# Two layers of cross attention on one core: transposes of the probabilities moved ahead of the filling matmuls, their copies between the two heads of a pair

## What is computed

```python
q = x @ Wq + bq; k = ctx @ Wk + bk; v = ctx @ Wv + bv          # layer 0
attn = softmax(q k^T * 16 ** -0.5 + mask)                       # 32 heads
y = layernorm(attn v @ Wo + bo + x) * gamma + beta
a = layernorm(ctx)                                              # layer 1
out = y + tanh(gate) * (softmax((y Wq) (a Wk)^T * 32 ** -0.5) (a Wv)) Wo
```

## Time and profile before

| | |
|---|---|
| median of 3 runs | 1230.87 us (1230.49 to 1233.23) |
| profiled execution: time / span | 1232.87 us / 1231.1 us |
| PE busy | 1151.5 us (94% of the span) |
| PEld busy | 942.6 us (77%) |
| DVE busy | 806.0 us (65%) |
| ACT busy | 749.8 us (61%) |
| POOL busy | 251.5 us (20%) |
| mean granted TensorE clock | 0.990 |
| DMA | 153.77 MB, mean 125 GB/s |

### The profile page before, as it was taken

One profiled execution on the slowest core, in us unless ns is written; L12 is line 12 of the kernel. 1 busy time (PEld: TensorE's weight loads), 2 busy tenths in 40 slices (PEclk: granted clock), 3 DMA queues, 4 the chain that ended last, 5 costly groups with the idle time before them and its releaser, 6 DMA issues.

```text
span 1231.1 us, 32229 instructions
## 1 busy us (share of the span) xinstructions
PE 1151.5 (94%) x10003; PEld 942.6 (77%) x10003; DVE 806.0 (65%) x2386; ACT 749.8 (61%) x2163; POOL 251.5 (20%) x264
## 2 busy tenths in 40 slices
PE   4989999999999999999999999999999999999997
PEld 4678778786877778787777878778787877878786
DVE  4365666767576776757677675766767586676735
ACT  3374656747475674747567474765747476574744
POOL 1041212111131211113121121312122131211210
PEclk9699999999999999999999999999999999999999
DMA  7665536547363654726365472735647273564500
GB/s 237 163 181 112 155 74 151 133 97 189 72 161 85 139 143 88 196 67 167 86 132 151 88 194 59 174 89 121 156 93 184 63 171 84 125 166 92 142 8 8
DMA packets 77821, 153.77 MB, mean 125 GB/s; under 512 B 10384, under 2 KB 47056, under 8 KB 77152
## 3 DMA queue, kind: packets, MB, share of 16 engines
q1 hardware_dynamic: 77792, 153.40, 51.3%
HBM read 113.72 MB, written 39.65 MB: 125 GB/s over the span
## 4 chain that ended last, share of the span: by engine, by line
PE 72%; issue 13%; ACT 6%; DVE 4%; DMA 1%; POOL 1%; DVEq 1%; ACTq 1%; SPq 0%; POOLq 0%
PE PJ L363 16%; PE TP L414 13%; PE OA L434 5%; PE SCO L400 5%; PE SCO L680 5%; PE SCO L458 4%; PE PJ L466 4%; ACT PR L1050 4%; PE PJ L376 4%; PE SCO L404 4%; PE OA L439 3%; PE SCO L363 2%; DVE SCO L824 2%; ACT PT L1061 1%; PE SCO L665 1%
## 5 line engine op out<-in xcount | busy, mean ns | idle before, releaser
L1050 ACT ACTIVATE PR<-SCO,MN 100x361 f32<-100x361 f32 x768 | 426.5, 567 | 144.8 <-DVE MN L824 143.2
L824 DVE CUSTOM_DVE_ANT_0 SCO<-SCO,MK 100x361 f32<-100x361 f32 x768 | 399.7, 551 | 126.0 <-PE SCO L400 99.7
L414 PEld LDWEIGHTS TP<-ident,PR 100*128 100x128 f32 x2304 | 222.5, 141 | 79.4 <-ACT PT L1061 28.5
L414 PE MATMUL TP<-ident,PR 100*128 100x100 f32 x2304 | 270.0, 253 | 6.7 <-ACT PT L1061 4.4
L1061 ACT ACTIVATE PT<-TP 121x600 f32<-121x600 f32 x256 | 172.2, 672 | 57.1 <-PE TP L414 55.1
L400 PE MATMUL SCO<-K0S,Q0S 128*100 128x362 f32 x512 | 165.8, 374 | 37.4 <-ACT PR L1050 36.1
L1050 ACT ACTIVATION_READ_ACCUMULATOR PR<-SCO,MN 100x1 f32 x768 | 159.7, 208 | 0.0
L834 DVE COPY PT<-TP 121x600 f32<-121x600 f32 x128 | 100.2, 783 | 65.6 <-PE TP L414 62.0
L400 PEld LDWEIGHTS SCO<-K0S,Q0S 128*100 128x100 f32 x512 | 74.8, 167 | 62.3 <-ACT PR L1050 60.0
L824 DVE DVE_READ_ACCUMULATOR2_ANT MN<- 100x1 f32 x768 | 108.5, 141 | 0.0
L1215 POOL TENSOR_TENSOR K1F<-K1F,KB 128x364 f32<-128x364 f32 x64 | 50.8, 794 | 259.8 <-DVE K1F L816 259.8
(11 more groups left out here) (140 smaller groups left out, 1814.8 us busy)
## 6 DMA issues: line engine op xcount, KB each, us to landing
K1S<-k_scr SPq DMA_DIRECT2D x128, 364.0 KB, 6.1
k_scr<-K1HL SPq DMA_DIRECT2D x64, 364.0 KB, 3.2
Q0S<-q_scr SPq DMA_DIRECT2D x128, 100.0 KB, 4.0
K0S<-k_scr SPq DMA_DIRECT2D x64, 182.0 KB, 5.0
AT<-ctx_cols SPq DMA_DIRECT2D x16, 722.0 KB, 9.4
V<-ctx_rows SPq DMA_DIRECT2D x16, 484.0 KB
q_scr<-QHL SPq DMA_DIRECT2D x16, 400.0 KB, 2.5
k_scr<-K1HL SPq DMA_DIRECT2D x32, 182.0 KB, 3.0
```

Of the source, the lines that this page charges most:

```text
L414: last = pe.transpose(TP[:, k % 2, c * T:(c + 1) * T], PR[0:T, k % NPR, c * SP:c * SP + P], ident[0:T, 0:T])
L824: dve.tensor_tensor_reduce(out=bank, in0=bank, in1=mask[0:T, :], scale=scale, scalar=3.4e38, op0=ALU.add, op1=ALU.min, accum_out=MN[0:T, k ...
L1050: act.activation(PR[0:T, k % NPR, 0:S], SCO[0:T, k % 3, 0:S], ACT.Exp, bias=MN[0:T, k:k + 1], scale=-1.0, accum_out=SM[0:T, k:k + 1]).then ...
```

## The change

1. PE, layer 0: the transposes of pair p-2 are issued directly behind the two scores of step p, ahead of its filling.
2. PE, layer 1: the second score of a step directly follows the first, then come the transposes, then the K1 matmuls.
3. DVE: its copies stand between the two shifts of a step, and one step earlier in the program (pair p-2 in step p), so that the copy of pair 21 is in step 23 of its own batch. The scalings K1F of steps 0, 3, 17 and 20 stand behind both shifts.
4. ACT: the copy of pair p-3 in layer 0 stands between the two exponentials of step p. The cast of chunk 3 of the keys moves from step 4 to step 5.
5. The bias of the layer-0 values is added by ACT in `values0_copied`, where it is one value per partition (BV0C, loaded by a DMA of its own at the start, counted by l_sm). The write to V0P is then a plain copy (`values0_out`) on ACT, ahead of its two Q1S copies; DVE no longer has it, and waits for the transposed values (v0_tr) ahead of K1F of chunk 0 instead.

```diff
         ROWS = sb("ROWS", [P, P + 3 * D + 1])
-        BV0, BO0, G0, B0 = (ROWS[:, 0:P], ROWS[:, P:P + D], ROWS[:, P + D:P + 2 * D], ROWS[:, P + 2 * D:P + 3 * D])
+        BO0, G0, B0 = ROWS[:, P:P + D], ROWS[:, P + D:P + 2 * D], ROWS[:, P + 2 * D:P + 3 * D]
...
+        BV0C = sb("BV0C", [P, 1])
...
             sp.dma_start(COLS[:, :], columns).then_inc(l_sm, 16)
+            sp.dma_start(BV0C[:, :], rows[0:P].rearrange("(p o) -> p o", o=1)).then_inc(l_sm, 16)
...
                         score(b, k)
+                    if p >= 2:
+                        transpose_probs(b, p - 2)
+                    elif not first:
+                        transpose_probs(b - 1, NPAIR - 2 + p)
                     if p in PV1_TAIL and not first:
...
                         out1(b - 1, range(*OUT1_STEPS[p]))
-                    if p >= 2:
-                        transpose_probs(b, p - 2)
-                    elif not first:
-                        transpose_probs(b - 1, NPAIR - 2 + p)
...
                     score(b, 2 * p)
+                    if p > 16:
+                        pe.wait_ge(prob, NH * b + 2 * p - 1)
+                    if p == 16:
+                        pe.wait_ge(rep_dve, 2 * b + 1)
+                    elif p == 17:
+                        pe.wait_ge(rep_dve, 2 * b + 2)
+                    score(b, 2 * p + 1)
+                    if p >= 18:
+                        transpose_probs(b, p - 2)
                     if more and p in K1_EARLY:
...
                     elif not more:
                         repeated_keys(3)
-                    if p > 16:
-                        pe.wait_ge(prob, NH * b + 2 * p - 1)
...
-                    score(b, 2 * p + 1)
...
-                    if p >= 18:
-                        transpose_probs(b, p - 2)
...
-            def values0(q, bank=PJ[:, 1, :]):
-                dve.wait_ge(v0_tr, q + 1)
-                dve.tensor_tensor(V0P[0:SP, :, :, HD0:2 * HD0],
...
                 if m == 0:
+                    dve.wait_ge(v0_tr, b + 1)
                     dve.wait_ge(rs_ev, b + 1)
...
                 for p in range(L0P):
-                    if p % 4 == 0 and (p > 0 or not first):
-                        if p > 0:
-                            probs_out(b, p - 3)
-                        else:
-                            probs_out(b - 1, NPAIR - 3)
-                    elif p == 2 and not first:
-                        probs_out(b - 1, NPAIR - 1)
                     if first and p in (4, 6, 8, 10):
                         keys1_scaled(b, p // 2 - 2)
-                    elif not first and p == 0:
+                    shift(b, 2 * p)
+                    if p == 1 and not first:
+                        probs_out(b - 1, NPAIR - 1)
+                    elif p % 4 == 3:
+                        probs_out(b, p - 2)
+                    shift(b, 2 * p + 1)
+                    if not first and p == 0:
                         keys1_scaled(b, 2)
                     elif not first and p == 3:
                         keys1_scaled(b, 3)
-                    for k in (2 * p, 2 * p + 1):
-                        shift(b, k)
...
-                probs_out(b, 13)
...
-                if more:
-                    values0(b + 1)
                 dve.wait_ge(mk1_b, b + 1)
                 for p in range(L0P, NPAIR):
-                    if p in (20, 22):
-                        probs_out(b, p - 3)
                     shift(b, 2 * p)
+                    if p in (19, 21, 23):
+                        probs_out(b, p - 2)
+                    shift(b, 2 * p + 1)
                     if more and p == 17:
                         keys1_scaled(b + 1, 0)
                     elif more and p == 20:
                         keys1_scaled(b + 1, 1)
-                    shift(b, 2 * p + 1)
...
-                act.activation(V0T[:, :], bank[:, 0:SC * SP], ACT.Copy).then_inc(v0_t, 1)
+                act.activation(V0T[:, :], bank[:, 0:SC * SP], ACT.Identity, bias=BV0C[:, 0:1]).then_inc(v0_t, 1)
+
+            def values0_out(q, bank=PJ[:, 1, :]):
+                act.wait_ge(v0_tr, q + 1)
+                act.activation(V0P[0:SP, :, :, HD0:2 * HD0],
+                               bank[0:SP, 0:SC * P].rearrange("p (s h d) -> p s h d", s=SC, h=KVH), ACT.Copy)\
+                    .then_inc(v0_ev, 1)
...
                     if p > 0:
                         exps(b, 2 * p - 2)
+                        if p >= 3 and (p - 3) % 4 != 1:
+                            probs_out(b, p - 3)
+                        elif p == 1 and not first:
+                            probs_out(b - 1, NPAIR - 2)
                         exps(b, 2 * p - 1)
...
-                    if p >= 3 and (p - 3) % 4 != 1:
-                        probs_out(b, p - 3)
-                    elif p == 1 and not first:
-                        probs_out(b - 1, NPAIR - 2)
...
-                    elif not first and p == 4:
+                    elif not first and p == 5:
                         keys1_high(b, 3, first)
...
                     .then_inc(q1_h, 1)
+                if more:
+                    values0_out(b + 1)
                 for j in (0, 2):
```

More of the change, by code:

```diff
@@ L883, in _ @@
                 .then_inc(v0w_l, 1)
-            dve.wait_ge(l_sm, 16)
+            dve.wait_ge(l_sm, 32)
             for s in range(SC):
@@ L890, in _ @@
             queries0_low(0)
-            dve.wait_ge(pool_zero, 3)
             dve.wait_ge(l_row, 16)
-            values0(0, SCO[:, 2, :])
             dve.wait_ge(l_rp, 16)
@@ L1018, in _ @@
             batch(NB - 1, False, False)
-            probs_out(NB - 1, NPAIR - 3)
             repeat_sums(NB - 1, 2)
@@ L1090, in _ @@
             act.activation(flat(WK0h), V1_flat[:, 0:C * P], ACT.Copy).then_inc(k0w_h, 1)
-            act.wait_ge(l_sm, 16)
+            act.wait_ge(l_sm, 32)
             act.activation(BQ0, BQ0, ACT.Copy, scale=SCALE0).then_inc(w_q0b, 1)
@@ L1110, in _ @@
                     .then_inc(wv_g, 1)
+            act.wait_ge(pool_zero, 3)
+            values0_out(0, SCO[:, 2, :])
             act.wait_ge(pad_zero, 3)
```

## The result

The changed kernel takes 1279.01 us (median of 4 runs, 1277.97 to 1280.34) against 1231.84 us for the kernel before in the same comparison: ratio 1.039, 95% interval 1.037 to 1.040. It is 47 us slower; the forecast was 33 us slower, 1264 us, range 1228 to 1284.

What follows compares the result with a forecast made beforehand. TensorE was taken as the bound. Fourteen middle batches at 0.1+1.95 (28.7), plus batch 0 and the last, gave +32.9 on 1232.87: 1265.8, with the median 2.0 lower, 1264 us; range 1228 to 1284, own range 1236 to 1279.

Steps and rivals of the forecast that it cites:

- passage: Stretch of a batch between layer 0 and layer 1, 22.73 us with TensorE busy 22.69; forecast to stay at 22.7.
- TP's waits over 20 us: Sign: TensorE's transposes waiting for ACT's copy out of TP grow from 4.4 to over 20 us, three per layer-1 stretch.
- the wait of S(3) gone: Sign in layer 0, step 1: the wait at 1.2 after S(2), before head 3's score, is gone; step 1 lost 1.25.
- a wait in front of S(39): Sign in layer 1, step 19: a wait of near 1 us stands before the score of head 39.
- K1HL waiting for POOL: Sign in layer 1: ACT's cast K1HL waits for POOL, which starts after the later scaling K1F.
- Rivals A and B: A: head-chain delays vanish, 1217 us, chance 0.13. B: step losses change place and not amount, 1231 us, chance 0.06.
- Part 4: Layer 1: S(35) waits for S(32)'s chain, late K1F delays exp(36), transposes wait; +1.95 a batch, bounds +1.0 and +2.3.
- Part 3: Layer 0: cast in step 5 makes S(13) 0.75, T(4) another 0.3 late; layer 0 +0.1 a batch, -0.7 to +0.9.
- Part 1: Transposes ahead of the filling: F no longer covers their wait for ACT's copy of the pair before, in both layers.
- the 2.09 rule: Where ACT copies pair p-3, the step before must last 2.09 us or TensorE waits; layer-1 steps have 1.68 us.
- part 2: Copies between the heads: step 1's loss goes, shift(2p+1) waits for its step's transposes; step 3 loses 1.4, before 0.5.
- rival C: Late transposes and VectorE copies feed each other: 0.4 per fourth layer-0 pair, 1.6 a batch more, 1288 us; chance 0.13.
- Part 5: Bias of layer-0 values on ACT: TensorE's wait for V0P goes, S(35)'s wait replaces it: 0, at most +1 us once.

Runs made afterwards that it cites:

- e10: e3 with pair 21 copied by ACT in step 0, behind exp(46) and exp(47); 1213.90 us, ratio 0.985 to the kernel before.
- e6: The changed kernel with K1F of chunk 3 ahead of the shifts of step 3 and its cast in step 4; 1272.00 us, ratio 1.031.
- e5: e4 with layer 1's transposes behind three of the K1 matmuls of their step; 1267.58 us, ratio 1.027.
- e9: e5 with VectorE's layer-1 copies taken from between the shifts, ahead of them one step later, pair 21's at batch end; 1251.45 to 1254.88 us, ratio 1.017.
- e3: The kernel before with only the bias of the layer-0 values moved to ACT; 1228.30 us, ratio 0.998.
- e7: The changed kernel with the reciprocals and spread of the sums behind the shifts of step 2 instead of step 1; 1278.38 us, ratio 1.036.
- e8: e3 with pair 21's transposes amid the output products of step 23 and VectorE's copy at the end of the batch; 1222.90 us, ratio 0.991.
- e1: The changed kernel with layer 1 in its old order on PE and VectorE, pair 21 copied last in the batch; 1241.05 us, ratio 1.008.
- e12: e10 with pair 23 also copied by ACT, and pair 1's and 5's transposes issued inside the output products; 1203.66 us, ratio 0.976.
- e4: The changed kernel with the scalings K1F of steps 17 and 20 between the two shifts; 1266.76 us, ratio 1.029.

## Why the prediction was right, and where not

| us | forecast | measured |
|---|---|---|
| layer 0, a middle batch | +0.1 | +0.79 |
| passage | 0 | -0.22 |
| layer 1 | +1.95 | +2.60 |
| 14 middle batches | +28.7 | +44.4 |
| start and batch 0 | +2.45 | -1.4 |
| last batch | +1.8 | +2.2 |
| sum, profiled executions | +32.9 | +45.1 |

- **The side and the mechanism were right.** All signs named at the end of the prediction appeared: TP's waits over 20 us, the wait of S(3) gone, a wait in front of S(39) (0.72, where "near 1 us" was said), K1HL waiting for POOL. Only the passage is 22.51 instead of 22.7. Rivals A and B fell: layer 0 did not get shorter, and the losses grew instead of changing place. That the gap ahead of S(3) was VectorE's order and no lack of buffers shows in e10: with the same buffers S(3) comes 2.00 after S(0), for 2.91 before.
- **The size was less good.** The median, 1279.0, is the upper end of the forecast's own range (1236 to 1279). The middle batches alone came 15.7 us above their forecast, and the start and batch 0 3.9 below theirs. That second miss is luck (see the last point but one): with the start as forecast the time would have been near 1283, an estimate from these numbers.
- **Part 4, layer 1, was 0.65 too low.** S(35) was put at 1.92 after S(32) and came at 1.94. Step 19 was to end 1.25 late and ended 1.34 late. With 0.33 for T(19), S(46) was to be 1.58 late and was 1.97 late (13.39 after S(32) for 11.42). The 0.33 is below the prediction's own rule, which gives 2.09-1.70 = 0.39. And T(19) started 2.59 after S(40), not 2.48: exp(40) stood behind exp(39), whose shift VectorE had made only behind its copy of pair 17. The last 0.28 is a cost I hadn't looked for. With the output products last in the batch instead of the transposes, S(0) is idle for "issue" where the loop jumps back: batch 14, the last of the loop, has a layer 1 of 16.42, and the batches before it 16.70.
- **Part 3, layer 0, was 0.7 too low**, inside its own bounds (-0.7 to +0.9). Up to step 6 it holds: S(14) was put 0.25 later than before and is 0.23 later. The 0.7 that is missing builds up in steps 8 to 15, which the prediction carried on step by step: S(20) was to be 0.05 later and is 0.39 later, the end of layer 0 was to be 0.1 later and is 0.79 later. No run split these steps. The sum hid larger terms: a gain of 0.9 for pair 21 (the prediction had it, as step 1), a loss of 1.7 for the order. The cast was sized at 0.75 and 0.3 where it costs 0.44 (e6); its place was right.
- **Part 1, the 2.09 rule**, describes the trace (125 waits of 0.16 us), but the length of these waits isn't what can be won back: with matmuls put in their place layer 1 stays as long (e5). The coupling through VectorE, which I had put into part 2 for step 3 and into rival C for an added loss, costs layer 1 0.85 a batch (e9, measured with the transposes behind three matmuls). I had played C through for layer 0 only.
- **Part 5, bias at nothing**, was wrong by 0.26 a batch in the change's favour (e3).
- **Start and batch 0** went the other way, by less than they vary. The changed kernel, e6 and e7 have the same program in batch 0, and yet the first score of batch 1 stands at 132.3, 133.5 and 135.5 us. Batch 0's own layer 1 became 1.64 longer (17.71 to 19.35), where 1.95 was forecast.
- The Trainium skill, Perfetto Trace Analysis, section Matmuls, says that independent groups should rotate through PSUM banks. Here that would be a second place for the pairs in TP, and the trace has 20.6 us of waits for it. No run gave TP a second place: the kernel's other PSUM tensors (SCO 3 banks, OA 1, PJ 2) and TP's 2 are eight in all. e5 only covered the waits and e9 moved VectorE's copy, which brought 12 us without a further bank. What earlier transposes with a second place would bring stays open.

## What to carry to other kernels

Where queues are in order, look at what stands behind a waiting instruction before you move the thing it waits for: a copy that waits for the newest product of another engine is harmless behind the critical work, and ahead of it costs time in every step. A sum of small terms near zero can hide two large ones (0.9 and 1.7 in layer 0), so split gains and losses before believing it. And count both roles of a filling: it covers waits of the matmul behind it, and what is put ahead of it is no longer covered.

## What the runs showed of the hardware that I had not expected

- When a round of the loop ends on TensorE with output products (48 small matmuls, 24 in e8), the first score of the next round is idle for 0.21 to 0.34 us with "issue" as the releaser. This stands at all 13 jumps back of the loop in the changed kernel, e8 and e9. With the transposes last, as in the kernel before, e1, e3, e10 and e12, none of them has it. Whether it is the kind or the number of the last matmuls that matters, no run shows.
- The transposes in e4's layer 1 waited 0.5 us, those in e5's not at all, and its length differed by 0.09 us: idle time on the engine that everything runs at was no measure of what it cost.
